# Row maxima from a difference: positive part on ScalarE, sum and maximum on VectorE, scores in three PSUM banks

## The chip, the cores and the metric

The kernel runs on one core of a Trainium2 chip. The metric is the device time of one execution in microseconds (us). The kernel before takes 1557.63 us, the median of three runs (1556.99 to 1558.35).

## The reference

The input is 4 sequences of 1024 rows of 128 numbers. A block of attention and a feed-forward block follow each other, each with a layer norm ahead and a residual sum behind:

```python
x = queries                                   # (4, 1024, 128) float32
x = x + attn(layernorm(x), Wq, Wkv, Wout, bout)   # 16 heads of 64; rotary on the first 32 of each head
x = x + ffn(layernorm(x), U1, V1, b1, U2, V2, b2) # ((x@U1)@V1 + b1) -> gelu -> @U2 -> @V2 + b2
# in attn, for each of the 4 * 16 = 64 heads, q, k, v are (1024, 64):
sim  = q @ k.T * 64 ** -0.5                   # 1024 x 1024
attn = softmax(sim, axis=-1)                  # the kernel takes each row's maximum out ahead of exp
out  = attn @ v
```

## The kernel before, in words

**Tiling.** The 64 heads are worked through in 16 groups of 4 (`GH`). One iteration is one group: 32 steps (`STEPS`), 8 for each head; a step t has keys of one block of 128 and all 1024 queries, so step n of the whole kernel makes scores of 128 keys by 1024 queries. The first iteration and the last stand apart in the code, the 14 between are a loop. Before the loop stand the layer norm of the first sequence, the projections of the first group, the hand-over of queries and keys, and the first 12 units; behind it the rest of the feed-forward block.

**Maxima first.** The maximum of each query row is needed before exp. A *unit* u is the scores of 128 queries against all 1024 keys of a head in plain precision. It is made 12 steps (`LEAD`) ahead of the scores. TensorE makes it with two matmuls of 64 rows (L397), keys 0 to 511 and keys 512 to 1023, into the two banks of `M`; VectorE reduces 128x1024 to one column of `MX` (L603). After the 8 units of a head ScalarE copies `MX` to `MN` (L501) and a DMA on SyncE's queue puts that as a row into the matmul operand `QML` (L716), so that scores come out with the maximum taken off. `M` has one place: unit u + 1 waits until `max_read` says that unit u was reduced (L406).

**Scores.** For each step, and each half z of the queries, two matmuls (L376, L377) make 128x512 scores in one bank of `S`. `S` has four banks; half j = 2n + z waits for `exped` to be at least j - 3 (L375), that is for the exp of four halves before. ScalarE reads each bank with Exp into `PF` in SBUF (L515), and `exped` grows by one for each half.

**Values and sums.** TensorE multiplies `PF` by `V` into `O` (L388), 4 steps behind; GpSimd adds pairs of `PF` (L676), VectorE adds these to `SUM` (L610, L613). After each head ScalarE copies `O` to `OS` (L494, two instructions, in step kt = 2 of the next head, ahead of its exps). Every two heads the sums are turned into inverses (den tile, L322; L619), spread by DMA, and multiplied in (L625), and the output projection follows (out tile, L330; L539).

**Order on TensorE** is written out by hand in `pe_step`. A pair of steps (t even, then t + 1) is: values of two steps, the unit of t, scores of t (halves z = 0 and 1), a tile if t has one, scores of t + 1 (two halves), a tile if t + 1 has one, the unit of t + 1. Below, the two units of a pair are called U(e) and U(o), and the four halves of scores S(e,0), S(e,1), S(o,0), S(o,1). Tiles (projections `QK_AT` and `V_AT`, den, out) go through the one bank `TILE`, at the step numbers of lists at the top of the file.

**Order on ScalarE** is `act_step`: in each step perhaps `act_max`, perhaps the copy of `O`, the two exps, then what the tiles want (`act_tiles`, with `act_rot` three steps behind a rot tile). VectorE's is `dve_step`: tiles of the step before, invert, sum, norm, and the unit's reduction last. SyncE's queue carries the hand-over of queries and keys (`hand_over`, 4 DMAs for each head), the maxima and the sums, in the order of `HAND_ORDER`. Each engine works its instructions in this order.

**PSUM** has 8 banks, and all are used: `S` 4, `M` 2, `O` 1, `TILE` 1.

Of the kernel before, what the change touches and what calls it, by code (L numbers as in the profile page):

```python
# [15 lines left out]
P = 128  # L16
# [11 lines left out]
HAND = 4 * 16  # L28
# [10 lines left out]
QK_TILES = [(w, c, t) for w in "qk" for c in range(2) for t in ("rot", "pass")]  # L39
# [14 lines left out]
DOWN_AT = (12, 14, 16, 18, 21, 23)  # L54
# [51 lines left out]
def build(nc, x_d, wq_d, wkv_d, wout_d, bout_d, u1_d, v1_d, b1_d, u2_d, v2_d, b2_d, rope_d, ident_d, out_d):  # L106
    with ExitStack() as ctx:
# [34 lines left out]
        QML = QK[:, :, 3, :]  # L142
        V = sb("V", [P, GH, KT * DH], F32)
# [8 lines left out]
        SUM = sb("SUM", [P, 2, N], F32)  # L152
        ONES = sb("ONES", [P, 32], F32)
# [4 lines left out]
        OS = sb("OS", [P, 2, 2, HALF], F32)  # L158
        MX = sb("MX", [P, 2, KT], F32)
# [18 lines left out]
        HB = [S[:, side, z * 512:(z + 1) * 512] for side in range(2) for z in range(2)]  # L178
        OB = [O[:, :], M[:, 0:512]]
        TB = [T[:, :], M[:, 512:1024]]  # L180
# [11 lines left out]
        added = sem("added")  # L192
        handed = [sem(f"handed{h}") for h in range(GH)]
        unit_made, max_read, max_found, max_row = (sem(n) for n in ("unit_made", "max_read", "max_found", "max_row"))
# [19 lines left out]
        def freed(kind, args, it):  # L214

            if kind == "proj":
                w, c, t = args
                g = it.i + 1
                if t == "rot":
                    return rot_read, g * 4 + "qk".index(w) * 2 + c + 1  # L220
                if t == "pass":
                    return pass_lo, g * 4 + "qk".index(w) * 2 + c + 1
# [170 lines left out]
        def pe_unit(e, u, place, q, bank):  # L393

            for c in range(2):
                rows, keys = slice(DH * c, DH * c + DH), slice(c * 512, (c + 1) * 512)
                mm = e.matmul(bank[:, keys], QHH[rows, place, q:N:KT], (KHL, KMH)[c][rows, place, keys],  # L397
                              start=True, stop=True)
            mm.then_inc(unit_made, 1)

        def pe_next_unit(e, it, u):

            place, q = (u // KT) % GH, u % KT
            if q == 0:
                e.wait_ge(handed[place], HAND * (it.i + u // STEPS + 1))
            e.wait_ge(max_read, it.step(u))  # L406
            pe_unit(e, it.step(u), place, q, M[:, :])
# [17 lines left out]
        def act_tile(e, kind, args, made, g, bank):  # L425

            if kind == "proj" and args[2] == "pass":
                w, c, _ = args
                e.wait_ge(tile_made, made)
                if w == "q" and c == 0:  # L430
                    for h in range(GH):
                        wait(e, handed[h], HAND * g)
# [10 lines left out]
        def act_rot(e, args, g):  # L443

            w, c, _ = args
            nth = "qk".index(w) * 2 + c
# [55 lines left out]

        def act_step(e, it, t):
# [4 lines left out]
            if kt == 2 and (not it.first or h > 0):  # L508
                act_copy_out(e, it.i * GH + h - 1, (h - 1) % GH)
            for z in range(2):  # L510
                e.wait_ge(scored, 2 * n + z + 1)
                if z == 0:
                    wait(e, pv_done, n - SLOTS + 1)
                    wait(e, two_summed, (it.i * GH + h - 1) * (KT // 2) + kt // 2 + 1)
                e.activation(PF[:, t % SLOTS, z * HALF:(z + 1) * HALF], S[:, t % 2, z * HALF:(z + 1) * HALF], ACT.Exp,  # L515
                             scale=EXP_SCALE).then_inc(exped, 1)
            act_tiles(e, it, t)


        def dve_tile(e, kind, args, made, g, bank):  # L520
# [4 lines left out]
            nth = "qk".index(w) * 2 + c  # L525
# [72 lines left out]
        def dve_max(e, u, head, place, q, bank):  # L598

            e.wait_ge(unit_made, u + 1)  # L600
# [26 lines left out]
        def dve_step(e, it, t):  # L627
# [15 lines left out]
            if not (it.last and u >= STEPS):  # L643
                dve_max(e, it.step(u), it.i * GH + u // KT, (u // KT) % GH, u % KT, M[:, :])


        def rot_add(e, args, g):

            w, c, _ = args
            nth = g * 4 + "qk".index(w) * 2 + c  # L650
# [28 lines left out]
        def pool_step(e, it, t):  # L679
# [55 lines left out]
        def sp_iteration(sp, it):  # L735
            for what, h in HAND_ORDER:
# [32 lines left out]
        def _(sp):  # L769
# [10 lines left out]
            sp.wait_ge(pass_lo, 4)  # L780
            sp.wait_ge(set_up, 3)
# [13 lines left out]
        def _(pool):  # L795
# [30 lines left out]
        def _(act):  # L826
# [36 lines left out]
            act.activation(B1[:, :], M[:, 0:FF // P], ACT.Copy).then_inc(b1_copied, 1)  # L863

            act_max(act, 0, 0)
# [34 lines left out]
        def _(pe):  # L900
# [18 lines left out]
            pe.transpose(M[:, 0:FF // P], B1R[:, :], IDENT[0:FF // P, 0:FF // P]).then_inc(b1_turned, 1)  # L919
            pe.wait_ge(b1_copied, 1)  # L920
            pe.wait_ge(set_up, 4)
            for u in range(LEAD):
                if u % KT == 0:
                    pe.wait_ge(handed[u // KT], HAND)
                wait(pe, max_read, u - 2)
                pe_unit(pe, u, u // KT, u % KT, (M[:, :], S[:, 0, :], S[:, 1, :])[u % 3])
            pe.wait_ge(max_read, LEAD)
# [45 lines left out]

            pe.wait_ge(max_read, END)
# [29 lines left out]
        def _(dve):  # L1004
# [30 lines left out]
            for u in range(LEAD):  # L1035
                dve_max(dve, u, u // KT, u // KT, u % KT, (M[:, :], S[:, 0, :], S[:, 1, :])[u % 3])
# [73 lines left out]
```

## Time and profile before

| what | value |
|---|---|
| median of 3 runs | 1557.63 us |
| the profiled execution's own time | 1557.27 us |
| its span, first to last instruction | 1555.5 us |
| TensorE busy | 1424.9 us, 92% |
| VectorE busy | 1222.0 us, 79% |
| GpSimd busy | 977.8 us, 63% |
| ScalarE busy | 778.3 us, 50% |
| mean granted TensorE clock | 0.986 |

The profiled execution lies 0.4 us under the median. Busy matmul time counts each matmul to its modelled end, and these overlap with the next matmul's start, so what TensorE costs is read from the distance between starts in the timeline. A time in square brackets behind a row is how long the engine sat idle before it and who ended that.

### The profile page before, as it was taken

Reading aid. Unit: us, or ns where it says so; the run is one execution under the profiler, and the core shown is the slowest. Engines: PE = TensorE matmul, PEld = TensorE weight load, DVE = VectorE, ACT = ScalarE, POOL = GpSimd, SP = SyncE. Lnnn points to the kernel's source line nnn. Section 1 sums busy time; section 2 is a strip of 40 time slices with the busy share of each in tenths; the row PEclk is TensorE's granted clock in tenths of the full one; section 3 lists DMA queues with packets and bytes.
Section 4 is the critical chain, followed back from the end, with each engine's and each line's share of the span. In section 5 each row is a group of like instructions: output and inputs, shape, how many; then the busy total and the mean of one; then the engine's idle time right before and its main releaser. Section 6 shows DMA issues by size and latency. Waiting matters only on the chain.

```text
span 1555.5 us, 25971 instructions
## 1 busy us (share of the span) xinstructions
PE 1424.9 (92%) x7289; PEld 546.8 (35%) x7289; DVE 1222.0 (79%) x1297; ACT 778.3 (50%) x1512; POOL 977.8 (63%) x501
## 2 busy tenths in 40 slices
PE   3689999999999999999999999999999999998886
PEld 1224333333333333333333333333333333333323
DVE  7787888788788878878788888878887887888744
ACT  3244554545454545555455454545545554544464
POOL 4388766658475665838476574848566584757731
PEclk9799999999999999999999999999999999999999
DMA  5312131221303121120313122031312204031002
GB/s 158 73 26 60 25 76 26 50 54 26 83 14 75 34 57 38 44 65 14 75 34 74 22 54 54 14 79 30 75 21 54 54 20 89 14 75 33 3 15 68
DMA packets 70209, 76.00 MB, mean 49 GB/s; under 512 B 27204, under 2 KB 36936, under 8 KB 69928
## 3 DMA queue, kind: packets, MB, share of 16 engines
q1 hardware_dynamic: 68736, 74.69, 21.4%
q10 hardware_dynamic: 1448, 1.00, 0.3%
q8 instruction: 13, 0.21, 0.1%
q14 instruction: 12, 0.10, 0.0%
HBM read 22.56 MB, written 2.36 MB: 16 GB/s over the span
## 4 chain that ended last, share of the span: by engine, by line
PE 56%; DVE 13%; issue 13%; POOL 7%; DMA 5%; ACT 3%; SPq 2%; DVEq 0%; ACTq 0%; POOLq 0%
PE O L388 18%; PE S L376 10%; PE S L377 8%; PE M L397 8%; DVE MX L603 5%; PE TILE L312 5%; DVE SUM L613 4%; DMA QK<-STAGE 4%; POOL SA L676 3%; PE TILE L322 2%; POOL STAGE L663 2%; ACT PF L515 2%; SPq L708 1%; PE TILE L306 1%; PE TILE L330 1%
## 5 line engine op out<-in xcount | busy, mean ns | idle before, releaser
L676 POOL TENSOR_TENSOR SA<-PF 128x1024 f32<-128x1024 f32 x256 | 616.5, 2424 | 372.5 <-DVE SUM L610 279.9
L515 ACT ACTIVATE PF<-S 128x512 f32<-128x512 f32 x1024 | 547.8, 599 | 564.9 <-PE S L377 564.1
L603 DVE TENSOR_REDUCE MX<-M 128x1 f32<-128x1024 f32 x504 | 614.5, 1219 | 229.3 <-PE M L397 229.1
L388 PE MATMUL O<-PF,V 128*64 128x512 f32 x2048 | 497.4, 607 | 0.0
L376 PE MATMUL S<-QK 128*128 128x512 f16 x1024 | 393.1, 384 | 0.0
L377 PE MATMUL S<-QK 128*128 128x512 f16 x1024 | 390.1, 381 | 0.0
L397 PE MATMUL M<-QK 64*128 64x512 f16 x1008 | 221.9, 437 | 65.9 <-DVE MX L603 47.7
L613 DVE TENSOR_TENSOR SUM<-SUM,SA 128x1024 f32<-128x1024 f32 x128 | 248.3, 1939 | 3.6 <-POOL SA L676 3.4
L397 PEld LDWEIGHTS M<-QK 64*128 64x128 f16 x1008 | 72.6, 140 | 370.8 <-DVE MX L603 247.9
L388 PEld LDWEIGHTS O<-PF,V 128*64 128x64 f32 x2048 | 124.5, 136 | 206.4 <-issue 149.8
L376 PEld LDWEIGHTS S<-QK 128*128 128x128 f16 x1024 | 99.9, 98 | 165.3 <-issue 64.2
L652 POOL TENSOR_TENSOR T<-T,ROPE 128x512 f32<-128x512 f32 x60 | 76.3, 1271 | 127.8 <-DVE T L532 127.8
L494 ACT ACTIVATE OS<-O 64x512 f32<-64x512 f32 x128 | 75.8, 592 | 130.8 <-PE O L388 130.0
L377 PEld LDWEIGHTS S<-QK 128*128 128x128 f16 x1024 | 100.7, 98 | 76.8 <-issue 1.4
L655 POOL TENSOR_TENSOR YR<-T 128x512 f32<-128x512 f32 x60 | 113.1, 1886 | 4.7
L663 POOL TENSOR_TENSOR STAGE<-YR,STAGE 128x512 f16<-128x512 f32 x64 | 97.7, 1526 | 21.1 <-ACT STAGE L451 21.1
L312 PE MATMUL TILE<-XT,WQK 128*128 (+1 forms) x372 | 102.4, 385 | 6.3 <-ACT V L441 2.6
L610 DVE TENSOR_TENSOR SUM<-SA 128x1024 f32<-128x1024 f32 x64 | 81.8, 1278 | 19.8 <-ACT DS L471 19.8
L330 PE MATMUL TILE<-WO,OS 128*128 (+1 forms) x504 | 68.9, 280 | 16.9 <-DVE OS L625 14.7
L625 DVE TENSOR_TENSOR OS<-OS,RB 128x1024 f32<-128x1024 f32 x32 | 78.7, 2460 | 6.4 <-DMA RB<-den 6.4
L330 PEld LDWEIGHTS TILE<-WO,OS 128*128 128x128 f32 x504 | 65.6, 194 | 31.5 <-issue 21.7
L539 DVE TENSOR_TENSOR X<-TILE,X 128x512 f32 (+1 forms) x63 | 43.2, 685 | 29.4 <-PE TILE L330 29.4
(96 smaller groups left out, 749.0 us busy)
## 6 DMA issues: line engine op xcount, KB each, us to landing
QK<-STAGE SPq DMA_DIRECT2D x128, 256.0 KB, 3.9
QK<-STAGE SPq DMA_DIRECT2D x128, 128.0 KB, 3.1
RB<-den SPq DMA_DIRECT2D x128, 128.0 KB, 3.0
X<-in_L_attn_queries SPq DMA_DIRECT2D x4, 512.0 KB, 12.8
RT<-DS SPq DMA_DIRECT2D x128, 2.0 KB, 1.7
out<-X SPq DMA_DIRECT2D x8, 256.0 KB, 2.3
WRAW<-in_L_attn_Wkv SPq DMA_DIRECT2D x1, 1024.0 KB, 8.7
ROPE<-in_rope SPq DMA_DIRECT2D x1, 1024.0 KB, 12.0
```

What stands on the lines that cost most here:

```text
L312: mm = e.matmul(bank, WQK[:, "qk".index(w), wp, kind, cols], XT[:, xp, rows], start=(n == 0), stop=(n == 2))
L330: mm = e.matmul(bank[:, j * P:(j + 1) * P], OS[:, parity, z, j * P:(j + 1) * P], WO[:, pair, :], start=True, stop=True)
L376: e.matmul(S[:, t % 2, rows], KHL[:, h, keys], QHH[:, h, rows], start=True, stop=False)
L377: e.matmul(S[:, t % 2, rows], KMH[:, h, keys], QML[:, h, rows], start=False, stop=True).then_inc(scored, 1)
L388: mm = e.matmul(O[DH * z:DH * z + DH, :], V[:, h, kt * DH:(kt + 1) * DH], PF[:, t % SLOTS, z * HALF:(z + 1) * HALF], start=(kt == 0), stop ...
L397: mm = e.matmul(bank[:, keys], QHH[rows, place, q:N:KT], (KHL, KMH)[c][rows, place, keys], start=True, stop=True)
L515: e.activation(PF[:, t % SLOTS, z * HALF:(z + 1) * HALF], S[:, t % 2, z * HALF:(z + 1) * HALF], ACT.Exp, scale=EXP_SCALE).then_inc(exped, 1)
L603: e.tensor_reduce(MX[:, place % 2, q:q + 1], bank, AX, ALU.max).then_inc(max_read, 1)
L613: e.tensor_tensor(SUM[:, h % 2, :], SUM[:, h % 2, :], SA[:, part - 1, :], ALU.add).then_inc(summed, 1)
L655: e.tensor_tensor(YR[:, :], T1[:, :], T2[:, :], ALU.add).then_inc(rot_sum, 1)
L663: e.tensor_tensor(LOW[w][:, 0, cols], YR[:, :], HIGH[w][:, 0, cols], ALU.subtract).then_inc(rot_lo, 1)
L676: e.tensor_tensor(SA[:, (t // 2) % 2, :], PF[:, t % SLOTS, :], PF[:, t % SLOTS + 1, :], ALU.add).then_inc(two_summed, 1)
```

## The change

It changes how a unit is made and read, and what banks the scores use. With a and b the scores of a query against keys 0 to 511 and 512 to 1023, max(a, b) = relu(a - b) + b.

- GpSimd makes `KDS`, the keys 0 to 511 less the keys 512 to 1023 (fp16, 128x1024 in one instruction at step 9), and `hand_over` gets two more DMAs for each head that put it into `KD`.
- TensorE's unit is again two matmuls of 64 rows and 512 columns: one with `KD` into the bank `MD` (one place), one with the keys 512 to 1023 into `MR0` or `MR1` by turns.
- ScalarE takes the positive part of `MD` into `LEFT` in SBUF (128x512; two places): ahead of the exps in even steps, behind exps and tiles in odd ones.
- VectorE adds `MR` and `LEFT` and takes the maximum in one instruction over 512 columns.
- The scores have three banks. Half z of an even step uses bank z; in an odd step z = 0 uses bank 2 and z = 1 bank 0. The wait on `exped` is 2n + z - 3 or 2n + z - 0.
- k is projected ahead of q; the tiles of projections and values move (`QK_AT`, `V_AT`), `NORM_AT` goes from 16 to 13, some tiles of the last iteration move. ScalarE's copy of `O` goes behind the exps of its step. Small inputs are put where `SA` is used later.

```diff
-HAND = 4 * 16
+HAND = 6 * 16
-QK_AT = (1, 3, 5, 7, 9, 11, 13, 15)
-V_AT = {8: (1, 0), 10: (1, 1), 22: (0, 0), 24: (0, 1)}
+QK_AT = (1, 3, 4, 7, 8, 10, 11, 13)
+KD_AT = 9
+V_AT = {14: (1, 0), 16: (1, 1), 22: (0, 0), 24: (0, 1)}
-NORM_AT = {16: 1, 26: 0}
+NORM_AT = {13: 1, 26: 0}
...
-        S = pb("S", [P, 2, N], F32)
-        M = pb("M", [P, N], F32)
+        S = pb("S", [P, 3, HALF], F32)
+        MD = pb("MD", [P, 512], F32)
+        MR = [pb(f"MR{n}", [P, 512], F32) for n in range(2)]
...
+        def bank_of(t, z):
+            return ((0, 1), (2, 0))[t % 2][z]
...  pe_scores
-                wait(e, exped, 2 * n + z - 3)
-                e.matmul(S[:, t % 2, rows], KHL[:, h, keys], QHH[:, h, rows], start=True, stop=False)
-                e.matmul(S[:, t % 2, rows], KMH[:, h, keys], QML[:, h, rows],
+                wait(e, exped, 2 * n + z - (0, 3)[t % 2 != z])
+                e.matmul(S[:, bank_of(t, z), :], KHL[:, h, keys], QHH[:, h, rows], start=True, stop=False)
+                e.matmul(S[:, bank_of(t, z), :], KMH[:, h, keys], QML[:, h, rows],
...
-            for c in range(2):
-                rows, keys = slice(DH * c, DH * c + DH), slice(c * 512, (c + 1) * 512)
-                mm = e.matmul(bank[:, keys], QHH[rows, place, q:N:KT], (KHL, KMH)[c][rows, place, keys],
-                              start=True, stop=True)
-            mm.then_inc(unit_made, 1)
+            wait(e, left_over, u)
+            wait(e, max_read, u - 1)
+            e.matmul(MD[:, :], QHH[0:DH, place, q:N:KT], KD[:, place, :], start=True, stop=True)
+            e.matmul(MR[side][:, :], QHH[DH:P, place, q:N:KT], KMH[DH:P, place, 512:N],
+                     start=True, stop=True).then_inc(unit_made, 1)
...
+        def act_left(e, u, side):
+            e.wait_ge(unit_made, u + 1)
+            wait(e, max_read, u - 1)
+            e.activation(LEFT[:, side, :], MD[:, :], ACT.Relu).then_inc(left_over, 1)
...  act_step
-            if kt == 2 and (not it.first or h > 0):
-                act_copy_out(e, it.i * GH + h - 1, (h - 1) % GH)
+            more = not (it.last and t + LEAD >= STEPS)
+            if t % 2 == 0 and more:
+                act_left(e, it.step(t + LEAD), t % 2)
             for z in range(2):
                 e.wait_ge(scored, 2 * n + z + 1)
...
+            if kt == 2 and (not it.first or h > 0):
+                act_copy_out(e, it.i * GH + h - 1, (h - 1) % GH)
             act_tiles(e, it, t)
+            if t % 2 == 1 and more:
+                act_left(e, it.step(t + LEAD), t % 2)
...  dve_max
-            e.tensor_reduce(MX[:, place % 2, q:q + 1], bank, AX, ALU.max).then_inc(max_read, 1)
+            e.wait_ge(left_over, u + 1)
+            e.sem_inc(max_begun, 1)
+            e.tensor_tensor_reduce(LEFT[:, side, :], MR[side][:, :], LEFT[:, side, :], 1.0, LOWEST, ALU.add, ALU.max,
+                                   MX[:, place % 2, q:q + 1]).then_inc(max_read, 1)
...
+        def pool_keys_less(e, g):
+            e.wait_ge(rot_hi, g * 4 + 2)
+            e.wait_ge(pass_hi, g * 4 + 2)
+            keys = HIGH["k"]
+            e.tensor_tensor(KDS[:, :, :], keys[:, :, 0:512], keys[:, :, 512:N], ALU.subtract).then_inc(keys_less, 4)
...  hand_over
+                sp.dma_start(KD[top, h, :], KDS[rows, t, :]).then_inc(handed[h], 16)
```

## Rows read from the trace of the kernel before

**Rows 1.** The page: span and busy time of each engine.
```profile
span 1555.5 us, 25971 instructions
PE 1424.9 (92%) x7289; PEld 546.8 (35%) x7289; DVE 1222.0 (79%) x1297; ACT 778.3 (50%) x1512; POOL 977.8 (63%) x501
```
**Rows 2.** Busy time by stretch; the third is one loop iteration.
```profile
core 0: us, PE busy (x) PEld busy (x) DVE busy (x) ACT busy (x) POOL busy (x), PEclk, DMA share, GB/s
30.00:57.00 27.00, 10.68 (x55) 3.78 (x56) 22.73 (x46) 3.21 (x7) 6.71 (x5) 0.63 0.57 117
...
691.96:781.50 89.54, 85.57 (x441) 32.62 (x442) 72.58 (x68) 45.92 (x90) 57.20 (x29) 1.00 0.21 47
...
1499.00:1523.00 24.00, 14.17 (x64) 4.40 (x63) 7.40 (x6) 14.60 (x24) 4.67 (x2) 0.83 0.08 23
```
**Rows 3.** Timeline, TensorE: start, length, instruction, idle before. The iteration's idle places.
```profile
697.79 0.44 PE L397 MATMUL M<-QK 64*128 64x512 f16 x2 [0.67 <-DVE MX L603]
...
723.13 0.82 PE L312 MATMUL TILE<-XT,WQK 128*128 x3 [0.19 <-ACT V L441]
...
739.20 1.15 PE L330 MATMUL TILE<-WO,OS 128*128 x8 [0.63 <-DVE OS L625]
...
743.37 0.44 PE L397 MATMUL M<-QK 64*128 64x512 f16 x2 [0.78 <-DVE MX L603]
...
749.27 0.44 PE L397 MATMUL M<-QK 64*128 64x512 f16 x2 [0.51 <-DMA QK<-STAGE]
...
768.42 0.44 PE L397 MATMUL M<-QK 64*128 64x512 f16 x2 [1.12 <-DVE MX L603]
```
**Rows 4.** Timeline of a pair of steps: unit, reduction, scores, exps, copies on ScalarE.
```profile
726.12 0.44 PE L397 MATMUL M<-QK 64*128 64x512 f16 x2
...
726.70 1.22 DVE L603 TENSOR_REDUCE MX<-M 128x1 f32<-128x1024 f32 x1 [0.51 <-PE M L397]
726.72 0.38 PE L377 MATMUL S<-QK 128*128 128x512 f16 x1
...
727.22 1.09 ACT L515 ACTIVATE PF<-S 128x512 f32<-128x512 f32 x2 [2.63 <-PE S L377]
...
727.59 0.38 PE L377 MATMUL S<-QK 128*128 128x512 f16 x1
...
727.80 0.38 PE L376 MATMUL S<-QK 128*128 128x512 f16 x1
...
728.19 0.63 ACT L451 ACTIVATE STAGE<-YR 128x512 f16<-128x512 f32 x1
...
728.71 0.21 ACT L501 ACTIVATE MN<-MX 128x8 f16<-128x8 f32 x1
728.81 1.08 ACT L515 ACTIVATE PF<-S 128x512 f32<-128x512 f32 x2
```
**Rows 5.** Timeline, ScalarE: four exps in a row; the two copies of O.
```profile
732.30 2.06 ACT L515 ACTIVATE PF<-S 128x512 f32<-128x512 f32 x4 [2.41 <-PE S L377]
...
720.20 1.20 ACT L494 ACTIVATE OS<-O 64x512 f32<-64x512 f32 x2 [1.83 <-PE O L388]
```
**Rows 6.** Timeline: from ScalarE's end to the weight load that waited for it.
```profile
710.52 0.60 ACT L471 ACTIVATE DS<-TILE 128x512 f32<-128x512 f32 x1 [0.31 <-PE TILE L322]
...
711.17 0.33 PEld L312 LDWEIGHTS TILE<-XT,WQK 128*128 x3 [0.33 <-ACT DS L471]
```
**Rows 7.** Groups of instructions by line: busy, mean ns of one, idle before.
```profile
L603 DVE TENSOR_REDUCE MX<-M 128x1 f32<-128x1024 f32 x504 | 614.5, 1219 | 229.3 <-PE M L397 229.1
L539 DVE TENSOR_TENSOR X<-TILE,X 128x512 f32 (+1 forms) x63 | 43.2, 685 | 29.4 <-PE TILE L330 29.4
```
**Rows 8.** Timeline of the start: first and last of the 12 units ahead of the loop.
```profile
41.76 0.65 PE L397 MATMUL M<-QK 64*128 64x512 f16 x2 [6.51 <-DMA QK<-STAGE]
...
52.78 0.65 PE L397 MATMUL S<-QK 64*128 64x512 f16 x2 [0.49 <-DVE MX L603]
```

More of the change, by code:

```diff
@@ L37 @@
 PRE_CHUNKS = KT // CHUNK
-QK_TILES = [(w, c, t) for w in "qk" for c in range(2) for t in ("rot", "pass")]
+ORDER = "kq"
+QK_TILES = [(w, c, t) for w in ORDER for c in range(2) for t in ("rot", "pass")]
 PROJ = QK_TILES + [("v", 0, c) for c in range(2)]
-QK_AT = (1, 3, 5, 7, 9, 11, 13, 15)
-V_AT = {8: (1, 0), 10: (1, 1), 22: (0, 0), 24: (0, 1)}
+QK_AT = (1, 3, 4, 7, 8, 10, 11, 13)
+KD_AT = 9
+V_AT = {14: (1, 0), 16: (1, 1), 22: (0, 0), 24: (0, 1)}
 DEN_AT = {6: 1, 20: 0}
 INVERT_AT = {9: 1, 23: 0}
-NORM_AT = {16: 1, 26: 0}
+NORM_AT = {13: 1, 26: 0}
 OUT_AT = {17: (1, 0), 19: (1, 1), 28: (0, 0), 30: (0, 1)}
@@ L158, in build @@
         OS = sb("OS", [P, 2, 2, HALF], F32)
+        LEFT = sb("LEFT", [P, 2, 512], F32)
         MX = sb("MX", [P, 2, KT], F32)
@@ L171, in build @@
         QT = QK[:, 3, :, :].rearrange("p a b -> p (a b)").bitcast(F32)
-        S = pb("S", [P, 2, N], F32)
-        M = pb("M", [P, N], F32)
+        S = pb("S", [P, 3, HALF], F32)
+        MD = pb("MD", [P, 512], F32)
+        MR = [pb(f"MR{n}", [P, 512], F32) for n in range(2)]
         O = pb("O", [P, HALF], F32)
         T = pb("TILE", [P, 512], F32)
-        HB = [S[:, side, z * 512:(z + 1) * 512] for side in range(2) for z in range(2)]
-        OB = [O[:, :], M[:, 0:512]]
-        TB = [T[:, :], M[:, 512:1024]]
+        HB = [S[:, 0, :], S[:, 1, :], S[:, 2, :], MR[0][:, :]]
+        OB = [O[:, :], MR[1][:, :]]
+        TB = [T[:, :], MD[:, :]]
         x_in = [sem(f"x_in{b}") for b in range(B)]
@@ L191, in build @@
         pass_hi, pass_lo, v_made = sem("pass_hi"), sem("pass_lo"), sem("v_made")
-        added = sem("added")
+        added, keys_less = sem("added"), sem("keys_less")
         handed = [sem(f"handed{h}") for h in range(GH)]
-        unit_made, max_read, max_found, max_row = (sem(n) for n in ("unit_made", "max_read", "max_found", "max_row"))
+        unit_made, left_over, max_begun, max_read, max_found, max_row = (sem(n) for n in ("unit_made", "left_over", "max_begun", "max_read", "max_found", "max_row"))
         scored, exped, pv_done, o_copied = sem("scored"), sem("exped"), sem("pv_done"), sem("o_copied")
@@ L391, in pe_values, with pe_unit @@
             mm.then_inc(pv_done, 1)
[L393 to L399 removed]
+        def pe_unit(e, u, place, q, side):
+            wait(e, left_over, u)
[3 more added lines that the diff above has]
+                     start=True, stop=True).then_inc(unit_made, 1)
         def pe_next_unit(e, it, u):
@@ L405, in pe_next_unit @@
                 e.wait_ge(handed[place], HAND * (it.i + u // STEPS + 1))
-            e.wait_ge(max_read, it.step(u))
-            pe_unit(e, it.step(u), place, q, M[:, :])
+            pe_unit(e, it.step(u), place, q, u % 2)
         def pe_step(e, it, t):
@@ L429, in act_tile @@
                 e.wait_ge(tile_made, made)
-                if w == "q" and c == 0:
+                if w == ORDER[0] and c == 0:
                     for h in range(GH):
@@ L596, in split_ff_weights, with dve_max @@
                                    ALU.subtract).then_inc(f_w_lo, 1)
-        def dve_max(e, u, head, place, q, bank):
-            e.wait_ge(unit_made, u + 1)
+        def dve_max(e, u, head, place, q, side):
             if q == 0:
                 wait(e, max_found, head - 1)
-            e.tensor_reduce(MX[:, place % 2, q:q + 1], bank, AX, ALU.max).then_inc(max_read, 1)
+            e.wait_ge(left_over, u + 1)
+            e.sem_inc(max_begun, 1)
+            e.tensor_tensor_reduce(LEFT[:, side, :], MR[side][:, :], LEFT[:, side, :], 1.0, LOWEST, ALU.add, ALU.max,
+                                   MX[:, place % 2, q:q + 1]).then_inc(max_read, 1)
         def dve_sum(e, head, h, part):
@@ L685, in pool_step @@
                     rot_add(e, args, it.i + 1)
+            if t == KD_AT and not it.last:
+                pool_keys_less(e, it.i + 1)
             if t % 2 == 0 and (not it.first or t > 0):
@@ L807, in _ @@
                     rot_low(pool, args, 0)
+                    if args[0] == "k" and args[1] == 1:
+                        pool_keys_less(pool, 0)
             ln_rstd(pool, 1)
@@ L862, in _ @@
             act.wait_ge(b1_turned, 1)
-            act.activation(B1[:, :], M[:, 0:FF // P], ACT.Copy).then_inc(b1_copied, 1)
-            act_max(act, 0, 0)
+            act.activation(B1[:, :], MR[0][:, 0:FF // P], ACT.Copy).then_inc(b1_copied, 1)
+            for u in range(LEAD):
+                act_left(act, u, u % 2)
+                if u == KT + 1:
+                    act_max(act, 0, 0)
             def body(e, it):
@@ L924, in _ @@
                     pe.wait_ge(handed[u // KT], HAND)
-                wait(pe, max_read, u - 2)
-                pe_unit(pe, u, u // KT, u % KT, (M[:, :], S[:, 0, :], S[:, 1, :])[u % 3])
-            pe.wait_ge(max_read, LEAD)
+                pe_unit(pe, u, u // KT, u % KT, u % 2)
             def body(e, it):
```

34 lines of the change are left out of this document (20 added, 14 removed).

## The prediction

> **What bounds the kernel now.** I read the page first: TensorE is busy 92% of the span, VectorE 79%, ScalarE 50% [rows 1]. A share over the span does not say what a microsecond on VectorE is worth, so the second view is busy time by stretch: one loop iteration lasts 89.54 us, in which TensorE is busy 85.57 and VectorE 72.58, at granted clock 1.00, its level of 2.4 GHz [rows 2]. The third view is TensorE's own timeline over that iteration, for the places where it sat idle. There are six: three before a unit that waited for VectorE's reduction, and one each for V's copy, for the norm and for the handed-over queries, 0.67 + 0.19 + 0.63 + 0.78 + 0.51 + 1.12 = 3.90 us [rows 3]. So TensorE, working in its written order, bounds the loop. What the change can win by relieving VectorE is at most these 3.9 us for each of 16 iterations, 62 us.
>
> The fourth view is one pair of steps [rows 4], because the change puts ScalarE's work for the unit, and a new wait on ScalarE, between TensorE's instructions. Times below are from the start of U(e), 726.12.
>
> **VectorE.** The reduction over 128x1024 takes 1.22 us [rows 7]. No row shows the sum with maximum. The nearest rows bound it: an addition of one PSUM and one SBUF operand over 512 columns, 0.69 us, and the reduction it replaces, 1.22 us [rows 7]. I take 0.7, being nearest in operands and columns; 32 units then free some 17 us of VectorE's 72.6 an iteration, and at 1.22 none. Neither end puts it on the path: `MR` and `LEFT` have two places each, so it may be nearly two units late. With that the three waits of units go; the wait for queries goes too (the last q tile is two steps earlier, and the iteration will be longer, which hides the two added DMAs of each head on SP's queue), and so do those for V's copy and the norm. I count all 3.9 us as won; the other bound is 0.
>
> **TensorE's instructions** stay as many and as large: two matmuls of 64 rows by 512 columns for each unit, four for each step's scores. Cost nothing, for they replace their likes.
>
> **GpSimd** gets one subtraction over 128x1024 an iteration at step 9. It is busy 57.20 of 89.54 us [rows 2], and the next thing wanted from it, the rotary sum of tile 11, is wanted three steps behind its tile. Nothing; if that cover were gone, the subtraction would delay one copy of ScalarE in an iteration, which the upper bound takes in.
>
> **ScalarE** gets 32 Relu an iteration. Four exps in a row take 2.06 us, one alone 0.60, so each further one costs (2.06 - 0.60) / 3 = 0.49 us [rows 5]: 16 us an iteration on an engine busy 45.9 [rows 2]. As a share that is harmless. No row shows a Relu; a Copy stands between Exps with no gap (0.63 us at 728.19, next start 0.52 later [rows 4]), so I price it at 0.49. The Trainium skill, ScalarE: Activation LUTs, section Table sets: the hidden batching unit, says that relu is in every set, so no table switch would be due; no row here shows that for Relu. It matters where these 0.49 us stand, and that is the next point.
>
> **The wait of the scores.** This decides. Banks by half are 0, 1, 2, 0. The new wait is 2n + z - 3 where t % 2 differs from z and 2n + z - 0 where they are equal. Even z = 0 needs the exp of the half just before (it has the same bank), and TensorE has values and a unit between. But odd z = 1 is equal too: S(o,1) waits for exped >= 2n + 1, and that is the exp of S(o,0), made directly before it. Its bank was last read by the exp of S(e,0), two halves earlier; the wait asks for more than the bank does. Nothing stands on TensorE between S(o,0) and S(o,1), not even a tile. So in each pair TensorE must finish S(o,0), ScalarE must see it and exp it, and only then does S(o,1) begin; behind it in TensorE's order stand the odd tile, U(o), all values and the next pair.
>
> Its price at least: from the second matmul of a half to its exp is 0.50 us (726.72 to 727.22 [rows 4]), the exp 0.60, from ScalarE's end to the weight load that waited 0.05 (710.52 + 0.60 to 711.17 [rows 6]), less the 0.21 to the next matmul's regular start (727.59 to 727.80 [rows 4]): 0.50 + 0.60 + 0.05 - 0.21 = 0.94 us. I worked out each of the 16 pairs by ScalarE's order:
> - Plain pair (t = 0, no even tile). Relu starts at 0.58, as VectorE's reduction did (726.70). Exp of S(e,0) 1.10, of S(e,1) 1.59, of S(o,0) 2.08, ended 2.68; S(o,1) at 2.73 where it was due at 1.68 (727.80): 1.05.
> - Pairs with an even tile (t = 4, 6, 8, 16, 20, 22, 24, 28, 30): the tile delays S(o,0) too and lets ScalarE catch up, so the least price stands, with what a copy of the tile adds: 0.97 on average, 9 pairs, 8.7 us. A tile between the pair's halves does not cover the wait.
> - t = 12: the copy of the maxima in front adds 0.10 (728.71 to 728.81 [rows 4]): 1.15. t = 14: V's copy 0.49 and a rotary copy 0.52, part of it under the tile: 1.5.
> - t = 2, 18, 26: the copy of O, two instructions of 1.20 us together [rows 5], now stands between the exps of the even step and the exp of S(o,0), and the overlap of neighbours, 0.11, is lost: 1.05 + 1.33 = 2.38, three times 7.1. t = 10, with a pass tile to copy as well: exps until 2.19, O until 3.41, tile copy until 3.90, exp until 4.50, S(o,1) 4.55 against 1.68 + 0.65 (three matmuls of 0.215): 2.2.
>
> Sum: 1.05 + 8.7 + 1.15 + 1.5 + 7.1 + 2.2 = 21.7 us an iteration.
>
> **The wait of ScalarE for the units.** Behind the Relu stand that step's exps. U(e) is made before the scores and U(o) behind them, in ScalarE's order too, so this costs no more than above. `MD` is read long before the next unit: between U(o) and U(e) stand the values of two steps.
>
> **The start.** 12 units ran from 41.76 to 52.78, 1.00 us each [rows 8]. With one `MD` each waits for the Relu of the one before: 0.65 [rows 8] + 0.14 (as VectorE's start behind a unit, 726.12 + 0.44 to 726.70 [rows 4]) + 0.60 + 0.05 = 1.44, so 11 x 0.44 = 4.8 us later. The added DMAs and the subtraction ahead of the first unit have no row of their own; they are in the bounds, 1 and 8.
>
> **The sum.** 1557.3 (profiled execution; 0.4 under the median) + 16 x (21.7 - 3.9) + 4.8 = 1557.3 + 284.8 + 4.8 = 1846.9. Say 1847 us, 18.6% more.
>
> **The rivals.**
> - *The clock falls with the waits* (0.10). The granted clock was 0.63 where TensorE was busy 10.68 of 27.00 us and 0.83 at 14.17 of 24.00; it was 1.00 at 85.57 of 89.54 [rows 2]. After the change it would be some 86 of 107, between the two. The Trainium skill, TensorE: Matmul & The Clock Gate, section A second HAM failure mode: psum-queue depth-cycling, tells of a kernel whose PE idled shortly and often between groups and went back and forth between its clocks. If the mean were 0.90, 85.6 us of dense work would become 95: 16 x 9.5 = 152 more, about 2000 us.
> - *The wait is mostly hidden* (0.09). If ScalarE sees matmuls sooner than the row says and the copies overlap, the least price 0.94 holds in all pairs and the four copies of O add half of theirs: 16 x (16 x 0.94 + 2.4 - 3.9) = 217, 1774 us.
> - *The other side: VectorE's relief counts and the wait does not* (0.05). Then the loop loses its six idle places and nothing comes: 1557 - 62 + 4 = 1499 us. This holds where the exp of S(o,0) has ended by the time TensorE comes to S(o,1). TensorE would have to come 0.94 us later than now, with other work between, and the order puts none there. Against it speaks the wait's own number.
> - *The sum with maximum is slow* (0.04). If the new instruction took over 3 us, VectorE would bound a loop of over 110 us: some 1900 and more. Both nearest rows speak against it.
>
> **How the numbers follow.** The forecast has 0.72. Its lower bound is the hidden wait's, rounded down to 1770; its upper bound takes nothing won and 0.1 us more for each pair: 1557 + 16 x (21.7 + 1.6) + 8 = 1938. From 1770 to 1938 leaves out the clock, the other side and part of the slow sum. A measurement of this kernel can tell 0.2% from no change, 3 us. Faster: the other side, 0.05. Same: only an accident between the cases, 0.01. Slower: 0.94.
>
> **What would show it.** TensorE's rows of the second half of odd steps would have an idle of about 1 us in front of them, ended by the exp, some 256 times, twice as long in four pairs of each iteration; that group's idle sum would be 250 to 370 us where the kernel before has none. An iteration would last about 107 us. VectorE's busy time falls by 270 us with no gain in time; no unit waits for it. ScalarE's busy time grows by 300 us. I am wrong if S(o,1) follows S(o,0) at 0.21 us, or if the granted clock in the loop is under 0.95.

## The result, and the profile after

The kernel after takes 1859.78 us (median of 4 runs, 1859.41 to 1860.65); beside it on the same chip the kernel before took 1557.99 us. The ratio is 1.193, 95% interval 1.191 to 1.195. Forecast were 1847 us and a range from 1770 to 1938. The profiled execution has a span of 1858.1 us, 302.6 more than before.

The page after, the parts that answer to [rows 1] and [rows 7]:

```profile
span 1858.1 us, 29110 instructions
PE 1498.0 (81%) x7289; PEld 537.3 (29%) x7289; DVE 900.9 (48%) x1809; ACT 1093.4 (59%) x2024; POOL 981.2 (53%) x517
...
L625 DVE CUSTOM_DVE_ANT_0 LEFT<-MR,LEFT 128x512 f32<-128x512 f32 x512 | 353.9, 691 | 820.0 <-ACT LEFT L517 811.3
L532 ACT ACTIVATE PF<-S 128x512 f32<-128x512 f32 x1024 | 581.0, 596 | 225.6 <-PE S L388 218.0
L387 PE MATMUL S<-QK 128*128 128x512 f16 x1024 | 397.4, 388 | 303.3 <-ACT PF L532 303.3
L517 ACT ACTIVATE LEFT<-MD 128x512 f32<-128x512 f32 x512 | 304.9, 595 | 458.5 <-PE MR L409 425.5
```

The work moves as the change says: VectorE is busy 321 us less, ScalarE 315 us more. What matters is the row of L387, the first matmul of each half of scores: TensorE sat idle 303.3 us in front of it, all of it ended by the exp, L532. The list of who waited for whom has the number of times: 256, once for each pair of steps.

```profile
PEld S L387 <- ACT PF L532: 455.9, 287, 2.8
ACT LEFT L517 <- PE MR L409: 425.5, 294, 6.8
POOL SA L706 <- DVE SUM L633: 416.0, 62, 11.3
PE S L387 <- ACT PF L532: 303.3, 256, 2.3
```

TensorE's timeline answers to [rows 4]; a pair with a tile in its even step, from U(e) at 841.30:

```profile
841.30 0.43 PE L408 MATMUL MD<-KD,QK 64*128 64x512 f16 x1
...
842.54 0.81 PE L319 MATMUL TILE<-XT,WQK 128*128 x3
843.19 0.38 PE L387 MATMUL S<-QK 128*128 128x512 f16 x1
843.40 0.38 PE L388 MATMUL S<-QK 128*128 128x512 f16 x1
844.70 0.39 PE L387 MATMUL S<-QK 128*128 128x512 f16 x1 [0.92 <-ACT PF L532]
844.93 0.38 PE L388 MATMUL S<-QK 128*128 128x512 f16 x1
```

S(o,0) is made at 843.19 and 843.40. S(o,1) would be due at 843.62 and starts at 844.70, 1.08 us late. The bracket says 0.92, because the matmul before counts to its modelled end; each bracket of this kind is short by 0.17. The pair before has the copy of O; here is ScalarE's side of it:

```profile
834.90 1.09 ACT L532 ACTIVATE PF<-S 128x512 f32<-128x512 f32 x2
836.01 1.19 ACT L504 ACTIVATE OS<-O 64x512 f32<-64x512 f32 x2
837.23 0.60 ACT L532 ACTIVATE PF<-S 128x512 f32<-128x512 f32 x1
...
837.88 0.39 PE L387 MATMUL S<-QK 128*128 128x512 f16 x1 [2.30 <-ACT PF L532]
```

Two exps of the even step, then the two copies, then the exp of S(o,0), and 0.05 us behind its end S(o,1).

Busy time by stretch answers to [rows 2] (columns as there):

```profile
841.30:948.66 107.36, 88.06 (x434) 31.34 (x432) 51.23 (x100) 64.66 (x120) 54.53 (x29) 0.97 0.18 42
```

The granted clock is 0.97 where it was 1.00. This stretch is 2.6 us short of an iteration: from one den tile of step 6 to the next it is 958.76 - 848.81 = 109.95 us, in which TensorE is busy 90.64, against 85.57 of 89.54 before. The iterations of the loop are by turns 110.0 and 108.5 us long, 109.3 on average over 13 of them (89.57 before, taken in the same way). The six idle places of [rows 3] are gone.

### The profile page after: what moved, and what is told of

Its sections match the earlier page's. It is cut to its first block, busy times and chain, and to the rows that moved or that the text cites. A ratio compares the mean times of both kernels' runs of the same rounds, so it can differ in the third digit from the quotient of the medians.

```text
span 1858.1 us, 29110 instructions
## 1 busy us (share of the span) xinstructions
PE 1498.0 (81%) x7289; PEld 537.3 (29%) x7289; DVE 900.9 (48%) x1809; ACT 1093.4 (59%) x2024; POOL 981.2 (53%) x517
## 3 DMA queue, kind: packets, MB, share of 16 engines
HBM read 22.56 MB, written 2.36 MB: 13 GB/s over the span
## 4 chain that ended last, share of the span: by engine, by line
PE 64%; ACT 18%; issue 11%; DVE 2%; ACTq 2%; POOL 2%; DMA 1%; SPq 0%; DVEq 0%; POOLq 0%
PE O L399 25%; ACT PF L532 12%; PE S L387 11%; PE MD L408 10%; PE S L388 8%; PE TILE L319 4%; ACT OS L504 4%; PE TILE L337 3%; PE TILE L329 2%; ACTq L219 1%; ACT LEFT L517 1%; POOL QK L835 1%; ACTq L528 1%; ACT STAGE L443 0%; ACT STAGE L461 0%
## 5 line engine op out<-in xcount | busy, mean ns | idle before, releaser
L625 DVE CUSTOM_DVE_ANT_0 LEFT<-MR,LEFT 128x512 f32<-128x512 f32 x512 | 353.9, 691 | 820.0 <-ACT LEFT L517 811.3
L532 ACT ACTIVATE PF<-S 128x512 f32<-128x512 f32 x1024 | 581.0, 596 | 225.6 <-PE S L388 218.0
L387 PE MATMUL S<-QK 128*128 128x512 f16 x1024 | 397.4, 388 | 303.3 <-ACT PF L532 303.3
L517 ACT ACTIVATE LEFT<-MD 128x512 f32<-128x512 f32 x512 | 304.9, 595 | 458.5 <-PE MR L409 425.5
L399 PE MATMUL O<-PF,V 128*64 128x512 f32 x2048 | 518.5, 629 | 0.0
L387 PEld LDWEIGHTS S<-QK 128*128 128x128 f16 x1024 | 99.3, 97 | 564.5 <-ACT PF L532 455.9
L408 PE MATMUL MD<-KD,QK 64*128 64x512 f16 x512 | 230.1, 449 | 15.7 <-ACT LEFT L517 9.1
L409 PE MATMUL MR<-QK 64*128 64x512 f16 x512 | 230.4, 450 | 0.0
L636 DVE TENSOR_TENSOR SUM<-SUM,SA 128x1024 f32<-128x1024 f32 x128 | 190.9, 1491 | 2.7 <-POOL SA L706 2.5
L408 PEld LDWEIGHTS MD<-KD,QK 64*128 64x128 f16 x512 | 71.8, 140 | 329.6 <-issue 285.6
L686 POOL TENSOR_TENSOR STAGE<-YR,STAGE 128x512 f16<-128x512 f32 x64 | 77.8, 1216 | 66.5 <-ACT STAGE L461 66.5
L319 PE MATMUL TILE<-XT,WQK 128*128 (+1 forms) x372 | 110.3, 409 | 3.0 <-DVE XT L1047 2.5
L409 PEld LDWEIGHTS MR<-QK 64*128 64x128 f16 x512 | 72.2, 141 | 0.0
```

The source lines that it names most:

```text
L319: mm = e.matmul(bank, WQK[:, "qk".index(w), wp, kind, cols], XT[:, xp, rows], start=(n == 0), stop=(n == 2))
L387: e.matmul(S[:, bank_of(t, z), :], KHL[:, h, keys], QHH[:, h, rows], start=True, stop=False)
L399: mm = e.matmul(O[DH * z:DH * z + DH, :], V[:, h, kt * DH:(kt + 1) * DH], PF[:, t % SLOTS, z * HALF:(z + 1) * HALF], start=(kt == 0), stop ...
L408: e.matmul(MD[:, :], QHH[0:DH, place, q:N:KT], KD[:, place, :], start=True, stop=True)
L409: e.matmul(MR[side][:, :], QHH[DH:P, place, q:N:KT], KMH[DH:P, place, 512:N], start=True, stop=True).then_inc(unit_made, 1)
L517: e.activation(LEFT[:, side, :], MD[:, :], ACT.Relu).then_inc(left_over, 1)
```

## The experiments

The theory on record: S(o,1) waits for the exp of S(o,0), made directly before it, and this wait, one in each pair, costs the time. Rivals: first, the new unit and ScalarE's 305 us of Relu; second, three banks being too few; third, that a wait for any late exp is as dear.

**e1_wait2: the wait that the bank needs.** One number is changed in the kernel after.

```diff
-                wait(e, exped, 2 * n + z - (0, 3)[t % 2 != z])
+                wait(e, exped, 2 * n + z - ((0, 3), (3, 2))[t % 2][z])
```

> The kernel after, with one number changed: S(o,1) waits for exped >= 2n + z - 2 (what its bank needs: the exp of S(e,0)) in place of 2n + z - 0. Theory (the wait on the exp of S(o,0) is the cause): nothing holds S(o,1), exp of S(e,0) ends at 1.70 us of the pair where S(o,1) is due at 1.68. TensorE's six idle places of the kernel before are gone (-62 us), the start costs 4.8 us, and in two pairs of an iteration the Relu of U(o), behind the copy of O, comes 0.4 to 0.6 us late for the next U(e) (+16 us): about 1516 us, between 1500 and 1530, granted clock in the loop 1.00 again. Rival (three banks and 305 us more work on ScalarE are too little and too much, whatever the wait's number): still above 1700 us.

Measured: 1568.76 us, ratio to before 1.0065 (1.0048 to 1.0082). 291 of 302 us are gone with this number, with three banks, the Relu and the new unit all in place. That settles the main question against the first two rivals; the third is left to e1_wait1. But 1516 was a miss: the gain of 4 us an iteration did not show. TensorE's own waits in this kernel:

```profile
PE TILE L319 <- DVE STAGE L556: 28.2, 29, 1.7
PE O L399 <- ACT OS L504: 15.2, 31, 1.0
...
PE S L387 <- ACT PF L532: 10.4, 13, 0.9
PE MD L408 <- ACT LEFT L517: 9.0, 13, 0.7
```

The first three rows, 54 us, are new idle places in the loop, nearly as much as the 62 us of the old ones. The fourth is not of the loop: 12 of its 13 places lie in the first 62 us, where the first units wait for one another's Relu, and the kernel after has it too (9.1 us). The longest new one is in each iteration the tile of step 11:

```profile
727.02 1.19 ACT L504 ACTIVATE OS<-O 64x512 f32<-64x512 f32 x2
728.24 0.60 ACT L443 ACTIVATE STAGE<-TILE 128x512 f16<-128x512 f32 x1
...
728.87 0.69 DVE L556 TENSOR_TENSOR STAGE<-TILE,STAGE 128x512 f16<-128x512 f32 x1 [1.94 <-ACT STAGE L443]
...
729.62 0.82 PE L319 MATMUL TILE<-XT,WQK 128*128 x3 [1.73 <-DVE STAGE L556]
```

The one bank `TILE` is still held by step 10's tile, since its copy on ScalarE stands behind the copy of O. In the kernel after, the wait for the exp hides this: S(o,1) is held first.

**e1_wait1: one half more than the bank needs.** The 2 above is a 1.

> The kernel after, with S(o,1) waiting for exped >= 2n + z - 1, the exp of S(e,1): one half later than its bank needs, one earlier than the change has. Theory: only the five pairs without an even tile wait, from 1.68 to 2.24 us, 0.56 us each: 5 x 0.56 x 16 = 45 us over e1_wait2, about 1560 us. In pairs with an even tile no wait. Rival (any wait on a late exp costs about a microsecond in each pair): about 1760 us.

Measured: 1591.84 us (2 runs), 23 more than e1_wait2; 45 were expected. TensorE's idle before L387 is 43.2 us in 79 places (10.4 in 13 in e1_wait2), so the waits are in the five pairs without an even tile, 5 x 16 = 80 in all, as said. Four of the five are 0.4 to 0.5 us in brackets and that of t = 0 is 1.3 to 1.4; behind the pair of t = 26 the values then wait 0.17 us for `O` instead of 0.66, so a part of the waits takes the place of other idle. A wait for the exp one half earlier costs 23 us, the change's wait 291. So a late exp is not dear in itself: this answers the third rival.

**e2_before_strict: the wait alone, in the kernel before.**

```diff
-                wait(e, exped, 2 * n + z - 3)
+                wait(e, exped, 2 * n + z - (3, 0)[t % 2 * z])
```

> The kernel before, with one part of the change alone: S(o,1) waits for exped >= 2n + 1 in place of 2n - 2. Four banks, VectorE's reduction over 1024 columns, no Relu, the copy of O ahead of the exps, as before. Theory: 8 pairs with an even tile 0.97 us, 5 plain ones 1.1, 3 with the copy of O 1.27: 17.1 us an iteration, less 3.9 us of idle places that this hides: 16 x 13.2 = 211, about 1769 us. Rival (the new way of making a unit, not the wait, costs the time): within 1% of 1558 us.

Measured: 1781.79 us, ratio 1.144 (1.142 to 1.146). With four banks, the old unit and no Relu, the wait costs 224 us; 211 were worked out. Its row is the same kind as in the kernel after:

```profile
PE S L376 <- ACT PF L515: 260.2, 256, 1.6
```

**e3_short_relu: 16 columns of Relu.** The maxima are not the true ones.

```diff
-            e.activation(LEFT[:, side, :], MD[:, :], ACT.Relu).then_inc(left_over, 1)
+            e.activation(LEFT[:, side, 0:16], MD[:, 0:16], ACT.Relu).then_inc(left_over, 1)
```

> The kernel after, with the Relu over 16 columns in place of 512, so that the maxima are not the true ones; the wait of S(o,1) stays as in the change. Theory: Relu ends as the exp of S(e,0) becomes possible anyway (1.07 against 1.10 us of the pair), so its length is nearly free: 1845 to 1862 us. Rival (ScalarE's added work, 305 us, is what makes the exps late): 150 us or more less than the kernel after.

Measured: 1857.17 us (2 runs), 2.6 under the kernel after. The Relu's length is free where it stands, with the change's wait in place.

**e4_short_copy: 16 columns of O.** The output is not the true one.

```diff
-                cp = e.activation(OS[rows, h // 2, z, :], O[DH * z:DH * z + DH, :], ACT.Copy)
+                cp = e.activation(OS[rows, h // 2, z, 0:16], O[DH * z:DH * z + DH, 0:16], ACT.Copy)
```

> The kernel after (strict wait kept), with the copy of O over 16 columns of each half in place of 512, so that the output is not the true one. The copy goes from 1.20 to some 0.4 us, in four pairs of an iteration. If the waits of 2.1 to 2.3 us there cost only their own length: 16 x 4 x 0.85 = 54 us less, about 1805 us. If they also make the granted clock fall (after two of them TensorE's next unit and values ran 1.5 us longer), another 3 us an iteration comes back and the loop's granted clock is 1.00: about 1757 us.

Measured: 1776.75 us (2 runs), 83 less: 5.2 us an iteration, between the two numbers. The idle before L387 falls from 303.3 to 251.4 us, 52, as the copies' own length says. The other 31 us fit what the clock gives back: from 172 to 1700 us of the kernel after the granted clock fell 21 times, and what it lacks to 1.00, summed over stretches of 1 us, is 36 us; in this one's loop it fell once, and the sum is 1.7. A stretch of 107 us of each (after, then this one):

```profile
595.00:702.00 107.00, 87.70 (x433) 31.23 (x433) 51.28 (x99) 65.44 (x122) 55.64 (x30) 0.98 0.18 42
```
```profile
595.00:702.00 107.00, 90.99 (x456) 32.45 (x457) 53.60 (x102) 63.65 (x125) 60.81 (x32) 1.00 0.19 43
```

**e5_wait2_copy_first: e1_wait2 with the copy of O ahead of the exps,** as in the kernel before.

```diff
+            if kt == 2 and (not it.first or h > 0):
+                act_copy_out(e, it.i * GH + h - 1, (h - 1) % GH)
             for z in range(2):
                 e.wait_ge(scored, 2 * n + z + 1)
...
-            if kt == 2 and (not it.first or h > 0):
-                act_copy_out(e, it.i * GH + h - 1, (h - 1) % GH)
             act_tiles(e, it, t)
```

> As e1_wait2, but the copy of O stands ahead of the exps of its step, behind the Relu. Then the exp of S(e,0) is late by the copy and S(o,1), which now waits for it, waits 1.35 us in three pairs and 0.7 in one; against that the values no longer wait 0.3 to 0.7 us for the copy. If the place of the copy matters as ScalarE's order says: 30 to 50 us more than e1_wait2's 1569, about 1607 us. If it does not: 1569 us within 5.

Measured: 1594.37 us (2 runs), 26 more than e1_wait2, where 30 to 50 were expected. TensorE's idle before L387 is 65.5 us in 75 places (10.4 in 13 in e1_wait2), while the values no longer wait for `O`: with the wait that the bank needs, it is the exp of S(e,0) that must be early, and the copy's place behind the exps is the better one.

**e6_tiles_back and e7_relu_first.** e1_wait2 with the lists of step numbers of the kernel before; e7 puts the Relu of U(o) ahead of the tiles' copies besides.

```diff
-QK_AT = (1, 3, 4, 7, 8, 10, 11, 13)
+QK_AT = (1, 3, 5, 7, 9, 11, 13, 15)
-V_AT = {14: (1, 0), 16: (1, 1), 22: (0, 0), 24: (0, 1)}
+V_AT = {8: (1, 0), 10: (1, 1), 22: (0, 0), 24: (0, 1)}
-NORM_AT = {13: 1, 26: 0}
+NORM_AT = {16: 1, 26: 0}
-DOWN_AT = (12, 18, 21, 22, 23, 24)
+DOWN_AT = (12, 14, 16, 18, 21, 23)
...  e7 only, in act_step
+            if t % 2 == 1 and more:
+                act_left(e, it.step(t + LEAD), t % 2)
             act_tiles(e, it, t)
-            if t % 2 == 1 and more:
-                act_left(e, it.step(t + LEAD), t % 2)
```

> As e1_wait2, with the tiles, the norm and the down tiles at the step numbers of the kernel before (k still ahead of q). In e1_wait2 the tile of step 11 waits 1.73 us for that of step 10, whose copy stands behind the copy of O on ScalarE, and step 8's 0.16 for that of step 7. If these two are what ate the gain: 16 x 1.9 = 30 us less, about 1539 us, under the kernel before. If the banks of scores or ScalarE's load are the limit: 1569 us.

Measured: 1610.41 us, ratio to before 1.034, 42 more than e1_wait2 where 30 less were expected. A miss that teaches: the wait at step 11 is gone, but others came, each longer than its like of [rows 3].

```profile
749.15 0.82 PE L319 MATMUL TILE<-XT,WQK 128*128 x3 [0.82 <-ACT V L451]
...
765.84 1.15 PE L337 MATMUL TILE<-WO,OS 128*128 x8 [1.00 <-DVE OS L648]
...
776.83 0.41 PE L408 MATMUL MD<-KD,QK 64*128 64x512 f16 x1 [2.19 <-DMA QK<-STAGE]
```

The unit made in step 20 waits 2.19 us for the handed-over queries (0.51 in [rows 3]); over the whole run these waits are 44.8 us in 16 places, against 7.2 in one in e1_wait2 and 17.0 in 16 in the kernel before. Against the kernel before there are six DMAs for each head in place of four, and q is projected last; against e1_wait2 the last q tile comes two steps later. So the moved tiles hide a hand-over that is otherwise late. Whether the two added DMAs or the order of k and q makes it late was not taken apart.

> As e6_tiles_back, with the Relu of U(o) ahead of what the tiles want of ScalarE in odd steps. U(e) then waits less for it, while the tile's bank comes free about 0.5 us later, which the next tile, two steps on, does not feel: 5 to 15 us less than e6_tiles_back. If no unit waits for a Relu there: the same within 3 us.

Measured: 1608.84 us (1605.75 to 1611.15), no difference from e6_tiles_back. As said of e1_wait2's fourth row, hardly a unit in the loop waits for a Relu: from 61 to 1450 us of e6_tiles_back it is 1.4 us in 2 places.

**e8_tile_ahead: e1_wait2 with the tile's copy ahead of the copy of O.**

```diff
+            act_tiles(e, it, t)
             if kt == 2 and (not it.first or h > 0):
                 act_copy_out(e, it.i * GH + h - 1, (h - 1) % GH)
-            act_tiles(e, it, t)
```

> As e1_wait2 (S(o,1) waits for what its bank needs, tiles as in the change), but in the step that has both, ScalarE copies the tile ahead of the copy of O. In e1_wait2 the tile of step 11 waited 1.73 us because the copy of step 10's tile stood behind the copy of O. If that order is what eats the gain there: 1.2 us less an iteration at the tile, 0.5 more where the values wait for O, about 1558 us. If not: 1569.

Measured: 1551.87 us, ratio to before 0.9956 (0.994 to 0.997), 17 under e1_wait2, where 11 were expected. TensorE's idle before L319 falls from 28.2 to 10.6 us, and the values' wait for `O` stays at 15.2: the 0.5 us more that was expected there did not come.

**e9_before_copy_late: the kernel before with the copy of O behind the exps,** and nothing else (the lines of e5's diff moved the other way).

> The kernel before, with one part of the change alone: the copy of O stands behind the exps of its step. In e1_wait2 values waited for it 15 us in all, in 31 places. If this is a cost of the place alone: about 1573 us. If it takes ScalarE's load of the change: 1558 us.

Measured: 1582.11 us, ratio 1.016 (1.014 to 1.017). The place of the copy alone costs the kernel before 25 us, more than the 15 expected: the values wait for `O` 8.4 us, and projection tiles wait 15.9 us for the copy of a V tile that now stands behind the copy of `O` (2.6 in the kernel before).

**e10_copy_on_dve: e1_wait2 with the copy of O on VectorE.**

```diff
             dve_tiles(e, it, t)
+            if kt == 2 and (not it.first or h > 0):
+                dve_copy_out(e, it.i * GH + h - 1, (h - 1) % GH)
```

`dve_copy_out` has the waits and the two halves of `act_copy_out`, as tensor copies; ScalarE's call in the steps is gone.

> As e1_wait2, with the copy of O moved from ScalarE to VectorE, ahead of its reduction in step kt = 2: two instructions of some 0.7 us on an engine that is busy 55 of 90 us. If ScalarE's order is what is late in e1_wait2 (tile of step 11, values that wait for O, units that wait for a Relu: 28 + 15 + 9 us of TensorE's idle), most of it goes: about 1529 us, between 1515 and 1545, under the kernel before. If VectorE becomes late instead: 1569 or more.

Measured: 1518.11 us, ratio to before 0.975 (0.973 to 0.977). This beats both kernels, the one before by 39 us. The three rows of e1_wait2 that lie in the loop fall from 54 to 9 us: 28.2 to 9.0 before L319, and 15.2 and 10.4 to nothing. The last of these was ScalarE's late start at the turn of the loop, which is gone here too (see the last section). An iteration is 86.5 us long, and a stretch of 87 us is nearly full:

```profile
594.00:681.00 87.00, 86.44 (x445) 32.31 (x443) 60.64 (x111) 59.13 (x114) 58.93 (x29) 1.00 0.22 52
```

**e11_dve_strict: e10 with the change's wait put back.**

```diff
-                wait(e, exped, 2 * n + z - ((0, 3), (3, 2))[t % 2][z])
+                wait(e, exped, 2 * n + z - (0, 3)[t % 2 != z])
```

> As e10_copy_on_dve (1518 us), with the change's own wait put back: S(o,1) waits for the exp of S(o,0). Nothing else differs, and no copy of O stands between the exps. By the prediction's working: 10 pairs with an even tile 0.97 us, four plain ones 1.07, step 14's 1.5, step 0's 1.9 (its Relu comes late at the loop's turn, as the trace of the kernel after shows): 17.4 us an iteration, of which some 2 hide other idle places: 16 x 15.4 = 246, about 1764 us, granted clock in the loop 1.00. If the wait had only been dear because of the copy of O: under 1600 us.

Measured: 1738.09 us, 220 more than e10_copy_on_dve. 246 were expected. The wait alone is dear without any copy of O; in this kernel it stands 256 times with 213.4 us in brackets. Some 10 of the 26 us that are missing are step 0's pair: 1.9 us had been taken from the kernel after, and 0.99 + 0.17 = 1.16 came (0.17 is what the bracket leaves out).

## Why the prediction was right, point by point

- **The bound.** TensorE in its written order bounds the loop: right. VectorE's 321 us bought nothing by themselves.
- **The wait of the scores.** Named by its place, count and price, and right in each. The forecast said 21.7 us an iteration, 347 us in all. The trace has 303.3 us in brackets, and 256 x 0.17 for the modelled ends, 347. That the two agree to the microsecond is in part luck: an iteration of the loop has 22.0, the first 19.0 and the last 20.1. By pairs, the bracket plus 0.17: an even tile 0.86 to 1.09, 0.93 on average (0.97 was taken), t = 12 1.14 (1.15), t = 14 1.37 (1.5), t = 10 2.10 (2.2), t = 2, 18, 26 2.47, 2.40 and 2.26 (2.38).
- **The one pair that was mis-sized** is t = 0: 1.05 was worked out, and 1.76 + 0.17 = 1.93 measured. At the turn of the loop ScalarE came late to its first instruction, with nothing it waited for:

```profile
935.15 0.43 PE L408 MATMUL MD<-KD,QK 64*128 64x512 f16 x1
...
936.62 0.60 ACT L517 ACTIVATE LEFT<-MD 128x512 f32<-128x512 f32 x1 [2.52 <-issue]
937.12 1.57 ACT L532 ACTIVATE PF<-S 128x512 f32<-128x512 f32 x3
...
938.74 0.39 PE L387 MATMUL S<-QK 128*128 128x512 f16 x1 [1.76 <-ACT PF L532]
```

  The Relu started 1.47 us behind U(e) where 0.58 was taken. The small overestimates elsewhere made up for most of it. One term was added up wrongly: for the pairs with the copy of O the parts named, 1.20 and 0.11, give 2.36 and not 2.38, 1 us in all.
- **VectorE.** 0.7 us was taken for the new instruction; it took 0.69, with a second one of 0.08 that reads the maximum out and had not been foreseen. The units' work on VectorE fell by 228 us (from 623.9 to 396.4), and not by the 270 that were forecast. That VectorE's total fell by 321 comes from other instructions that ran shorter, above all the sums of L613, now L636: 1.94 us each before, 1.49 after. Why was not tested. Neither number bears on the time.
- **The gain of 3.9 us an iteration** was taken as won, and it was: an iteration of the loop is 109.3 - 89.6 = 19.7 us longer with 22.0 us of waits and some 2.5 us of lower clock in it, so some 5 us went elsewhere, among them the six idle places. But the step "all idle places go" holds only as long as the wait hides what else is late; e1_wait2 shows that the change's own order on ScalarE brings new ones, 54 us of them. As a statement on what the change could gain without its wait (the rival at 1499 us) it was wrong: 1569 us.
- **The clock.** It was a rival, at a mean of 0.90 and 2000 us; what came is a small part of it, 0.97 to 0.98 in the loop. The forecast had none, and here it was short by some 31 (what e4 gave back) to 36 us (what the granted clock lacks over the loop). So an iteration of the loop lasts 109.3 us and not about 107.
- **How near the number came** is in part luck. The 14 iterations of the loop grew by 276 us where 249 were forecast, 27 more; the first and the last grew by 22 us together where 36 were, 14 less; the start and the rest are within 1 us. That leaves the 13 us between 1847 and 1860. Of the 14 us, 4 are shorter waits; the rest was not taken apart.
- **The start.** 4.8 us were worked out; the first scores start at 61.2 us in place of 56.8: 4.4.
- **The Relu's function.** That it changes nothing for the exps had no row; now it has one. Above, an exp starts 0.50 us behind the start of a Relu, as one exp does behind another (0.49).
- **GpSimd, the DMAs and the Relu's place:** priced at nothing, and no wait for them shows in the loop of the kernel after (e3 shows the Relu's length), though e6 shows that the hand-over is late where the tiles are not moved.

The spans add up: start 4.4, first to last score 298.2 (1740.3 against 1442.1), the tail less than 0.1, together 302.6.

## What to carry to other kernels

A wait on a count that stands one item behind another is a full round trip between two engines, here 0.9 us or more each time, and no share of busy time shows it coming: write for each reuse of a buffer which item had it last, and wait for that number and no more. When an engine in the middle of a chain gets new work, look at what stands ahead of the instruction that others wait for; moving the copy of O behind the exps cost 25 us in one kernel and won 26 in another, and giving it to an engine with room won 51, of which some 10 was a late start of ScalarE that nobody had looked for. A gain read from idle places is an upper bound, until the order that replaces them has been walked through for new ones.

## What the runs showed of the hardware that was not expected

**The granted clock fell at single waits of 1.7 to 2.3 us, but not at each.** In this iteration of the kernel after it fell twice, each time at one of the long waits with the copy of O:

```profile
918.42 0.39 PE L387 MATMUL S<-QK 128*128 128x512 f16 x1 [2.09 <-ACT PF L532]
918.96 0.64 PE L408 MATMUL MD<-KD,QK 64*128 64x512 f16 x1
922.76 0.43 PE L408 MATMUL MD<-KD,QK 64*128 64x512 f16 x1
...
946.34 0.61 PE L387 MATMUL S<-QK 128*128 128x512 f16 x1 [2.30 <-ACT PF L532]
947.16 1.49 PE L319 MATMUL TILE<-XT,WQK 128*128 x3
948.58 0.65 PE L408 MATMUL MD<-KD,QK 64*128 64x512 f16 x1
951.24 0.43 PE L408 MATMUL MD<-KD,QK 64*128 64x512 f16 x1
```

From U(o) over the values to the next U(e) are 3.80 us, where 2.24 is usual (839.06 to 841.30 in the same trace): 1.56 more. The second time, from S(o,1) to U(e), 4.90 against 3.42. The stretch from 946.34 to 949.00 has a granted clock of 0.50, which is the lower of the two levels, 1.2 GHz, where 2.4 is the upper. By longer stretches, the one before the first fall and the one with it:

```profile
908.20:914.90 6.70, 5.95 (x37) 2.24 (x36) 3.21 (x8) 3.79 (x7) 3.95 (x2) 1.00 0.76 183
914.90:921.60 6.70, 4.61 (x18) 1.49 (x18) 4.12 (x6) 4.53 (x8) 2.45 (x2) 0.80 0.00 0
```

Not every such wait does it: the same copy's pair at 837.88, also with 2.30, was followed by matmuls at granted clock 1.00 (837.88 to 841.30). There the clock had fallen one pair before, at 830, behind the wait of t = 0, which is only 1.78 us. In the kernel's loop from 172 to 1700 us, read in stretches of 1 us, there are 21 falls: 18 at the waits of 2.09 and 2.30 (t = 26 and t = 2), 3 behind the 1.78 or 1.79 of t = 0, and none at the 2.23 of t = 18 (or the 1.93 of t = 10), though e3_short_relu has 3 of its 22 there. The iterations of 110.0 us have two falls, those of 108.5 one. Where the longest waits of the loop are shorter, falls are rare: one in e4_short_copy (behind 1.78), two in e1_wait2 (behind 1.73 and 1.74), none in e2_before_strict (at most 1.6) and e11_dve_strict (at most 1.2). So shorter waits go with fewer falls, but the length of the wait alone does not say when one comes, and what else does is not shown here.

The Trainium skill, TensorE: Matmul & The Clock Gate, section A second HAM failure mode: psum-queue depth-cycling, tells of a kernel in which short and frequent idle times between groups of matmuls made the clock go back and forth between its two levels. The trace agrees in this, at some 2.5 us an iteration of 109.

**ScalarE was late at the turn of the loop, but only in some kernels.** In the kernel after, the first Relu behind each of the 13 turns comes 1.47 us behind its unit, with no wait that the profile shows (the row at 936.62), and TensorE waits for it. In e1_wait2 this is the row of 10.4 us in 13 places. In e11_dve_strict, where the copy of O is VectorE's, the same Relu comes 0.55 us behind its unit (772.99 to 773.54) and there is no such idle; nor is there in the kernel before. The profile's queue of instruction transfers differs in the same way. Queue, packets, MB and share, in the kernel after and in e11_dve_strict:

```profile
q14 instruction: 80, 0.66, 0.1%
```
```profile
q14 instruction: 15, 0.12, 0.0%
```

It has 80 packets in all nine kernels with both the Relu and the copy of O on ScalarE, and these are the ones in which it was late; 15 in e10 and e11; 12 in the kernel before, e2 and e9. That is 65 more for 13 turns, five each. This fits a ScalarE that waits at the turn for its own instructions, but no run changed the length of its loop alone, so the cause is not shown.
